# Expert attention of a four-stage model on one core: norm spread over three engines, lead-in and tail reordered

## What is computed

```python
ss = sigmoid(x @ Ws).reshape(b, t, H, E); sd = sigmoid(x @ Wd).reshape(b, t, H, E)
ms, md = topk_mask(ss, 3), topk_mask(sd, 3)
q = einsum('bthed,bthe->bhtd', q5, sd * md)       # q5, k5, v5: x @ Wq, x @ Wkv
k = einsum('bthed,bthe->bhtd', k5, ss * ms)
v = einsum('bthed,bthe->bhtd', v5, ss * ms)
out = softmax(q * DH ** -0.5 @ k.T) @ v
o5 = einsum('bthd,dm->bthm', out, Wo).reshape(b, t, H, E, DIM)
y = einsum('bthem,bthe->btm', o5, md)
x = layernorm(x + y)                              # (x - mean) / sqrt(var + 1e-5)
```

## Time and profile before

| | us |
|---|---|
| median of 3 runs | 2145.1 |
| the profiled execution | 2147.77 |
| its span, first to last instruction | 2145.9 |
| lead-in of the expert attention (end of the block before to the first exponential, L669) | 279.5 to 362.4 |
| its 32 periods | 362.4 to 1368.0 |
| its tail (to the flag) | 1368.0 to 1423.2 |

### The profile page before, as it was taken

One profiled execution on the slowest core, in us unless ns is written; L12 is line 12 of the kernel. 1 busy time (PEld: TensorE's weight loads), 2 busy tenths in 40 slices (PEclk: granted clock), 3 DMA queues, 4 the chain that ended last, 5 costly groups with the idle time before them and its releaser, 6 DMA issues. The chain is left out here.

```text
span 2145.9 us, 25496 instructions
## 1 busy us (share of the span) xinstructions
PE 1807.0 (84%) x8678; PEld 817.6 (38%) x8678; DVE 1255.9 (59%) x2012; ACT 1245.2 (58%) x2372; POOL 892.6 (42%) x446
## 2 busy tenths in 40 slices
PE   5667718999999989999899999546999999999386
PEld 2323315544555444554445453112233332333143
DVE  5898949797667877688777566222213313120277
ACT  0000012676776666776666767604999999999232
POOL 3333311687876777767777678700000000000000
PEclk9988759999999999999999999756999999999688
DMA  1000010000000000000000000013220302200001
GB/s 37 10 10 0 0 32 10 19 19 10 19 19 19 10 19 10 19 19 10 19 10 19 19 10 1 0 31 118 70 75 34 111 28 79 79 20 21 21 30 39
DMA packets 28345, 60.50 MB, mean 28 GB/s; under 512 B 4210, under 2 KB 14900, under 8 KB 28212
## 3 DMA queue, kind: packets, MB, share of 16 engines
q1 hardware_dynamic: 28212, 58.81, 8.4%
HBM read 37.83 MB, written 18.87 MB: 26 GB/s over the span
## 5 line engine op out<-in xcount | busy, mean ns | idle before, releaser
L549 POOL TENSOR_TENSOR b_psum<-b_psum,b_probs 128x1024 f32<-128x1024 f32 x192 | 460.3, 2397 | 195.9 <-ACT b_probs L669 189.6
L1784 ACT ACTIVATE c_probs<-banks 128x1024 f32<-128x1024 f32 x512 | 484.3, 1040 | 72.0 <-PE banks L1836 49.1
L1022 DVE TENSOR_TENSOR b_gated<-banks,b_g 128x480 f32<-128x480 f32 x512 | 313.3, 655 | 222.3 <-PE banks L764 217.4
L669 ACT ACTIVATE b_probs<-banks 128x1024 f32<-128x1024 f32 x256 | 254.1, 1018 | 243.5 <-PE banks L797 242.5
L764 PE MATMUL banks<-b_w,b_xh 128*128 128x480 f32 x1024 | 350.1, 397 | 32.8 <-DVE b_xl L967 17.0
L797 PE MATMUL banks<-b_qq,b_kk 64*128 64x512 f32 x1024 | 266.6, 628 | 34.6 <-DVE b_gated L1022 28.3
L1030 DVE TENSOR_REDUCE b_tok<-b_gated 128x192 f32<-128x960 f32 x256 | 281.4, 1138 | 0.5
L1851 PE MATMUL banks<-c_probs,c_vg 128*32 128x512 f32 x2048 | 277.4, 614 | 5.1 <-DVE c_acc L1946 3.3
L646 ACT ACTIVATE b_share<-b_o,b_picked 128x64 f32<-128x64 f32 x1120 | 278.3, 337 | 4.2 <-DVE b_o L1055 4.0
L829 PE MATMUL banks<-b_probs,b_tok 128*64 128x512 f32 x1024 | 255.9, 622 | 0.9 <-ACT b_probs L669 0.9
L764 PEld LDWEIGHTS banks<-b_w,b_xh 128*128 128x128 f32 x1024 | 193.8, 189 | 112.8 <-issue 57.0
(11 more groups left out here) (195 smaller groups left out, 1877.9 us busy)
## 6 DMA issues: line engine op xcount, KB each, us to landing
b_raw_w<-in_L_ffn_W SPq DMA_DIRECT2D x32, 480.0 KB, 3.2
c_heads<-c_split SPq DMA_DIRECT2D x24, 512.0 KB
c_keys<-c_heads SPq DMA_DIRECT2D x16, 512.0 KB, 3.7
c_queries<-c_heads SPq DMA_DIRECT2D x16, 512.0 KB, 4.7
c_heads<-c_split SPq DMA_DIRECT2D x8, 384.0 KB
a_xs<-in_L_attn_x SPq DMA_DIRECT2D x4, 512.0 KB, 3.8
d_xs<-r SPq DMA_DIRECT2D x4, 512.0 KB, 2.9
out<-d_yo SPq DMA_DIRECT2D x4, 512.0 KB, 3.2
```

The costliest lines, as they stand in the source:

```text
L549: nc.gpsimd.tensor_tensor(psum[:, par, :], prev, probs[:, i % 4, :], ALU.add).then_inc(psum_rdy, 1)
L669: nc.scalar.activation(probs[:, i % 4, :], score_b[i % 2], ACT.Exp).then_inc(exp_rdy, 1)
L1022: nc.vector.tensor_tensor(shape(gated[:, t % 2, j, :]), shape(proj_b[u % WAYS][:, 0:HALF_W]), g.unsqueeze(2).broadcast_to([P, 3, HD2, E]), ...
L1784: nc.scalar.activation(probs[:, step % 2, c, :, :], unit_b[u % NU], ACT.Exp, scale=float(HD) ** -0.5).then_inc(exp_rdy, 1)
```

## The change

- **Norm of batches 0 to 2**: VectorE does the statistics, the variance plus eps and the first guess (`moment_parts`, in h = 4 and 5). GpSimd does the Newton steps and a shift -mean * rs, 14 dependent steps on [128 x 8] (`inverse_roots`, in h = 6 after i = 3). ScalarE scales: eight activations out = Identity(rs * y + shift) (`finish_norm`, in h = 7 at p = 1).
- **Lead-in**: Wo is loaded behind the raw weights of heads 0 and 1, under a semaphore of its own. TensorE waits for nothing before it turns x, for Ws and Wd before the gates, and for the memsets before the keys. ScalarE copies the turned x, takes the gates' exponentials and splits x ahead of the casts of the weights; VectorE does its split ahead of the gates.
- **Tail**: the shares of head 31 are 40 `scalar_tensor_tensor` on VectorE, straight into z, each half released by itself. The ten steps go to ten different banks and to separate copies in the memory of probs and psum. The count of safe reciprocals comes ahead of the norm. The last norm stays wholly on VectorE.
- Five more semaphores for each of the two calls of `switch_attention`.

```diff
@@ -423,6 +423,7 @@
...
+        shift = sb("shift", [P, NT])
...
@@ -442,9 +443,11 @@
...
+        moments, newton, normed, z_last = map(sem, ("moments", "newton", "normed", "z_last"))
...
+        last_b = [ps[:, 2 + k, :] for k in range(6)] + [ps[:, k, :] for k in range(4)]
...
@@ -505,17 +516,18 @@
...
-                for e in range(E):
-                    at = DH * (e % 2)
-                    sp.dma_start(wo[at:at + DH, e // 2, :], I["L0_ffn_Wo"][:, e * D:(e + 1) * D]).then_inc(w_in, 16)
...
-                for n in range(3):
+                for n in range(2):
...
+                for e in range(E):
+                    at = DH * (e % 2)
+                    sp.dma_start(wo[at:at + DH, e // 2, :], I["L0_ffn_Wo"][:, e * D:(e + 1) * D]).then_inc(wo_in, 16)
+                weights(2, 2)
@@ -562,6 +574,8 @@
...
+                        if i == 3 and norm_last and h == 6:
+                            inverse_roots(b - 1)
@@ -569,12 +583,24 @@
...
+                def inverse_roots(b):
+                    pool.wait_ge(moments, MOMENT_STEPS * (b + 1))
+                    st = Steps(pool, newton, NEWTON_STEPS * b)
+                    var, half_step = tmp[:, 0, :], tmp[:, 1, :]
+                    for _ in range(3):
+                        st.link(nc.gpsimd.tensor_tensor(half_step, rs[:, :], rs[:, :], ALU.mult))
+                        st.link(nc.gpsimd.tensor_tensor(half_step, half_step, var, ALU.mult))
+                        st.link(nc.gpsimd.tensor_scalar(half_step, half_step, -0.5, 1.5, ALU.mult, ALU.add))
+                        st.link(nc.gpsimd.tensor_tensor(rs[:, :], half_step, rs[:, :], ALU.mult))
+                    st.link(nc.gpsimd.tensor_tensor(shift[:, :], mv[:, :, 0], rs[:, :], ALU.mult))
+                    st.done(nc.gpsimd.tensor_scalar(shift[:, :], shift[:, :], -1.0, None, ALU.mult))
+                    assert st.n == NEWTON_STEPS, st.n
...
-                for half in range(2):
-                    add_share(half, B * NH - 1, B - 1, NH - 1)
...
@@ -649,6 +675,12 @@
...
+                def finish_norm(b):
+                    act.wait_ge(newton, NEWTON_STEPS * (b + 1))
+                    for t in range(NT):
+                        nc.scalar.activation(out[:, b * NT + t, :], y[:, t, :], ACT.Identity, bias=shift[:, t:t + 1], scale=rs[:, t:t + 1]).then_inc(normed, 1)
@@ -695,17 +727,20 @@
...
+                        if p == 1 and h == 7 and norm_last:
+                            finish_norm(b - 1)
...
+                for r in range(2):
+                    turned_x(0, r)
+                for r in range(2):
+                    gate_exps(0, r)
+                split_x(0)
...
-                for work in (turned_x, gate_exps):
-                    for r in range(2):
-                        work(0, r)
-                split_x(0)
@@ -713,10 +748,13 @@
...
-                for t in range(0, NT, 2):
-                    gated_share(last_n, B - 1, NH - 1, (t, t + 1))
-                for k in range(OUT_STEPS):
-                    copy_out(B - 1, k)
+                for k in range(6):
+                    act.wait_ge(zT_ps, ZT0 + OUT_STEPS * (B - 1) + k + 1)
+                    n_rows = min(P, ED - k % 3 * P)
+                    nc.scalar.copy(last_z(k // 3)[0:n_rows, k % 3, :], last_b[k][0:n_rows, :]).then_inc(zT_sb, 1)
+                for half in range(2):
+                    act.wait_ge(zT_ps, ZT0 + OUT_STEPS * (B - 1) + 7 + half)
+                    nc.scalar.copy(last_y(half), last_b[6 + half]).then_inc(zT_sb, 1)
@@ -732,6 +770,7 @@
...
+                        pe.wait_ge(w_in, 16 * 2)
...
@@ -927,14 +967,13 @@
...
-                pe.wait_ge(w_in, 16 * (2 + E))
-                pe.wait_ge(clear, 2)
...
+                pe.wait_ge(clear, 2)
@@ -946,12 +985,31 @@
...
-                for k in range(OUT_STEPS):
-                    out_left(B - 1, k)
-                    project_out_step(B - 1, k)
-                out_left(B - 1, OUT_STEPS)
+                pe.wait_ge(mult, MULT0 + U * B * NH)
+                pe.wait_ge(exp_rdy, EXP0 + NT * B * NH)
+                pe.wait_ge(wo_in, 16 * E)
+                for k in range(6):
+                    half, c = k // 3, k % 3
+                    n_rows = min(P, ED - c * P)
+                    if c == 0:
+                        pe.wait_ge(z_last, ED // DH * 4 * (half + 1))
+                    for j in range(4):
+                        flat = z[:, (B - 1) % 2, 4 * half + j, :, :].rearrange("p e d -> p (e d)")
+                        last = nc.tensor.transpose(last_b[k][0:n_rows, j * P:(j + 1) * P], flat[:, c * P:c * P + n_rows], ident[:, :])
+                    last.then_inc(zT_ps, 1)
+                for half in range(2):
+                    pe.wait_ge(zT_sb, Z_COPIES * (B - 1) + 3 * half + 3)
+                    for c in range(3):
+                        n_rows = min(P, ED - c * P)
+                        last = nc.tensor.matmul(last_b[6 + half], wo[0:n_rows, c, :], last_z(half)[0:n_rows, c, :], start=(c == 0), stop=(c == 2))
+                    last.then_inc(zT_ps, 1)
+                for half in range(2):
+                    pe.wait_ge(zT_sb, Z_COPIES * (B - 1) + 7 + half)
+                    for j in range(4):
+                        last = nc.tensor.transpose(last_b[8 + half][:, j * P:(j + 1) * P], last_y(half)[:, j * P:(j + 1) * P], ident[:, :])
+                    last.then_inc(zT_ps, 1)
...
-                    turn_counts(nc, pe, judged, good, ident, turn_b[0:1, 0:P])
+                    turn_counts(nc, pe, judged, good, ident, last_b[2][0:1, 0:P])
...
@@ -1055,12 +1112,49 @@
...
-                def norm_parts(b):
+                def moment_parts(b):
...
-                    st = Steps(dve, norm_steps, ONE + NORM_STEPS * b)
-                    yield from layer_norm_parts(nc, st, y, out[:, bass.ds(b * NT, NT), :], stats, mv, rs, tmp)
-                    st.settle_apart()
-                    assert st.n == NORM_STEPS
+                    if b:
+                        dve.wait_ge(newton, NEWTON_STEPS * b)
+                        dve.wait_ge(normed, NT * b)
+                    st = Steps(dve, moments, MOMENT_STEPS * b)
+                    for half in range(2):
+                        for t in range(4 * half, 4 * half + 4):
+                            st.done(nc.vector.bn_stats(stats[:, t, :], y[:, t, :]))
+                        yield
+                    st.settle()
+                    for t in range(NT):
+                        st.done(nc.vector.bn_aggr(mv[:, t, :], stats[:, t, :]))
+                    yield
+                    st.settle()
+                    st.link(nc.vector.tensor_scalar(tmp[:, 0, :], mv[:, :, 1], LN_EPS, None, ALU.add))
+                    st.done(nc.vector.tensor_scalar(rs[:, :].bitcast(I32), tmp[:, 0, :].bitcast(I32), -0.5, float(0x5F3759DF), ALU.mult, ALU.add))
+                    assert st.n == MOMENT_STEPS, st.n
+                    yield
+                def last_shares(n):
+                    for half in range(2):
+                        dve.wait_ge(z_rdy[half], Z0 + n)
+                    dve.wait_ge(o_rdy, O0 + n + 1)
+                    b, h = n // NH, n % NH
+                    for t in range(NT):
+                        for e in range(E):
+                            nc.vector.scalar_tensor_tensor(z[:, b % 2, t, e, :], o[:, t, :], picked[:, b % 2, t, h * E + e:h * E + e + 1], z[:, b % 2, t, e, :], ALU.mult, ALU.add).then_inc(z_last, 1)
+                def last_norm(b):
+                    dve.wait_ge(normed, NT * b)
+                    dve.wait_ge(newton, NEWTON_STEPS * b)
+                    for half in range(2):
+                        dve.wait_ge(zT_ps, ZT0 + OUT_STEPS * b + 9 + half)
+                        some = slice(4 * half, 4 * half + 4)
+                        nc.vector.tensor_tensor(y[:, some, :], last_b[8 + half].rearrange("p (t c) -> p t c", t=4), x[:, b * NT + 4 * half:b * NT + 4 * half + 4, :], ALU.add).then_inc(y_rdy, 1)
+                    dve.wait_ge(y_rdy, 2 * b + 2)
+                    st = Steps(dve, norm_steps)
+                    layer_norm(nc, st, y, out[:, b * NT:(b + 1) * NT, :], stats, mv, rs, tmp)
+                    st.settle()
@@ -1074,7 +1168,7 @@
...
-                        waiting["norm"] = norm_parts(b - 1)
+                        waiting["norm"] = moment_parts(b - 1)
@@ -1099,21 +1193,18 @@
...
-                        if norm_last and h >= 4 and p % 2:
-                            next(waiting["norm"], None)
+                        if norm_last and h in (4, 5) and p % 2:
+                            next(waiting["norm"])
...
-                    if norm_last and h == NH - 1:
-                        for _ in waiting["norm"]:
-                            pass
...
+                split_x(0)
...
-                split_x(0)
@@ -1123,13 +1214,12 @@
...
-                for half in range(2):
-                    add_residual(B - 1, half)
-                for _ in norm_parts(B - 1):
-                    pass
```

(6 more changed lines are left out.)

14 lines of the change are left out of this document (9 added, 5 removed).

## The result

The changed kernel takes 2090.5 us in the median of four runs (2083.62 to 2095.73), against 2144.8 for the kernel before (four runs, 2138.58 to 2145.93): the ratio is 0.9746, 95% interval 0.9726 to 0.9767. That is 54.3 us less, where 48.5 were forecast, and 6.1 us under the forecast time of 2096.6. The profiled execution is the fastest of the four: 2083.62, span 2081.8, mean granted clock 0.942 (before: 2147.77, 2145.9 and 0.923).

The account below looks back on a forecast made before the run. No engine saturated throughout; TensorE bounds undisturbed heads, GpSimd the last ones. Lead-in 13.5, steady heads 20.9 and tail 14.1 sum to 48.5 us: 2147.8 to 2099.3 profiled, median 2096.6, range 2082 to 2115.

Parts of the forecast that it names:

- Cause of the long heads: Heads h = 6, 7, batches 1 and 2: GpSimd stretches VectorE's small norm steps, TensorE waits; moving them gains 23.9 us.
- GpSimd's steps: Norm in h = 6: 14 dependent steps on GpSimd at 0.36 us each, together N = 5 us (3.5 to 7).
- N - 3.5: Batches 1 and 2: TensorE's wait for the low weights (L538) queued behind GpSimd's steps, 1.5 us each, 3.0 in all.
- rival (e): GpSimd's norm steps are cheap, 3.5 us together: 4.5 us more gained, 2092 us; chance 12%.
- Rival (a): VectorE holds up GpSimd's small norm steps as GpSimd does VectorE's; at 2 us a step 2165.6 us, slower; chance 3%.
- Lead-in: Block start to first gating: no wait for Wo, reordered work, one collision of 2.1 us; gain 13.5 us (11 to 15.7).
- Last batch: Last heads: GpSimd is the bound, so its norm steps delay the last share of head 30 by 3.5 us (1.5 to 6).
- Tail: After the last shares: VectorE shares, separate banks, clock rising between two projections, earlier count; gain 14.1 us, semaphore clears charged 0.7.
- Rival (c): The clock stays at 1.2 GHz in the tail: 4.6 us less gained, 2101 us; chance 16%.
- (b): GpSimd's norm steps are merely dear, 0.55 us each, and ScalarE's eight activations outlast their cover: 2107 us; chance 17%.
- (d): Loads or both L538 hold the gates in the lead-in: up to 4 us less gained, 2100.5 us; chance 12%.
- (f): Idle time in h = 6 and 7 returns as another wait and the tail gains nothing: within 0.2%; chance 2%.

Follow-up runs that it names:

- `after_again`: The changed kernel, unchanged, timed again beside the kernel before on one chip: 2087.7 us, ratio 0.972.
- `last_roots_again`: Second run of the changed kernel with the 14 steps of batch 2's norm moved from GpSimd to VectorE in the last batch: 2081.4 us, ratio 0.9707.

## Why the prediction came out right, step by step

**Cause of the long heads: right.** With the small steps gone h = 6 and 7 fell to 29.4, and with GpSimd's sums cut short they fell there while VectorE kept all its work. 24.0 us came back in these four heads, the whole of the forecast's 23.9. L75 or L76 is still held in h = 5 (2.3 us in batches 1 and 2) and costs nothing there, as I had put it.

**GpSimd's steps: mis-sized, by 1.1 us.** N was put at 5 us and is 3.9, since a step costs 0.28 and not 0.36: the gap, 0.08, was lost in the difference of two large numbers (0.13), and the length is 0.20. That my lower end for the length, 0.19, lies so near it is luck: the copy's 238 ns less 56 columns at 2.02 ns is 0.125, not 0.19. The wait forecast as N - 3.5 came as 0.23 at N = 3.9, where that is 0.4, and as 6.87 at N = 10.7, where it is 7.2. With so small a wait nothing is left of the 3.0 us that were charged for batches 1 and 2. In this term rival (e), cheap steps, was nearer than the forecast.

**Rival (a) fell, but the argument against it was too broad.** GpSimd's steps run beside L1079 and L1087 of VectorE or beside nothing, and keep to 0.19 to 0.24. I had argued that GpSimd's sums keep to 2.35 to 2.46 whatever VectorE does; over all of them, that is not so (2.34 to 2.75, last section). None of the steps met a VectorE operation of the kind that holds GpSimd. Nor did a first call cost anything: the first `tensor_scalar` on GpSimd takes 0.20. The Trainium skill ("GPSIMD Engine Reference", Instruction dispatch) gives about 6 us for the first call of a freshly loaded routine; this trace doesn't show it here.

**ScalarE: hidden, as forecast, though over its bound.** The eight activations take 3.2 us against 2.0 to 2.9 (the 0.36 of the upper end came from no row; they take 0.40 each), and ScalarE's busy time in h = 7 goes from 21.3 to 24.3 us; the head stays at 29.4. On VectorE the same work cost 3.8 a head.

**Lead-in: right in its steps, 1.3 short in its sum.** First gating 28.7 us after the block's start, as forecast; one collision of 2.0 us, as forecast (L1043 takes 6.83 for eight, 4.81 in the kernel before, where nothing is beside it). The gain at this point is 13.2. But 12.25 is what arrives at the first exponential: between gating and exponential the kernel after takes 41.9 us, the one before 40.9. The clock is the likely cause. In this trace it is at 0.5 once more for 3.4 us, from 342.9, with TensorE busy throughout, shortly before the first exponential at 349.55. Of the nine traces with the new lead-in the five that have this dip reach the first exponential after 70.5 to 70.7 us, the four without it (`after_again` among them) after 69.0 to 69.2, which would be a gain of 13.6 to 13.8.

**Last batch: near in number, half right in its reason.** The delay, forecast as 3.5, is 2.9 in this trace (55.03 less 52.13) and 2.3 in the second (54.42). The steps do hold back GpSimd's last sum of head 30, from 22.7 to 25.95 us after that head's start, and through TensorE's row sums the work behind it. But GpSimd is not the engine that comes last in the trace I read: it idles 0.9 us for ScalarE's exponential before its last sum in the kernel before, and 0.7 in the kernel after. ScalarE's chain is about as long.

**Tail: mis-sized by 4.** The gain from GpSimd's last share of head 30 to the end was put at 14.1 net of the 3.5; it is 21.0 less 2.9, 18.1. Three pieces make up the 4.0. From the last share to the statistics I had 21.3 us (1379.6 to 1400.9) and it is 19.1: 2.2, and that is the clock. I let it rise between the two projections, 5.78 and then 2.9; it rose before both, and the twelve matmuls took 6.29, 2.4 less. The 40 shares were right (7.93 against 8.1), the transposes ended 0.7 earlier, the two rounds took 0.9 longer. The delay was 0.6 shorter. And from the statistics to the next block 2.3 us came back where I had 1.2, since the ten more semaphore clears, charged with 0.7, show in no run: from the flag to the next block it is 12.9 us before and 12.3 after. Rival (c), no rise, is refuted for this tail; with one bank both projections did run at 0.50.

**The other rivals.** (b) fell with N = 3.9 and h = 7 at 29.4, (d) with the first gating at 28.7, (f) with the four heads at 29.4 and the tail's gain.

**Sum.** 12.25 + 24.0 + 18.1 is 54.4, and h = 4, whose length varies from execution to execution (31.71, 34.11 and 35.09 in one trace of the kernel after, 34.74, 35.09 and 34.12 in the other), adds 0.4 in these two traces: 54.8. The three terms were 13.5, 20.9 and 14.1: one too large by 1.3, two too small by 3.1 and 4.0. So the mechanisms held, and the sum was 6 us too cautious, mostly by the wait charged to the steps and by the clock in the tail.

## What to carry to other kernels

Price a small VectorE instruction with its inputs in the memory that GpSimd uses by what GpSimd does beside it, not by its size; either give it to an engine that isn't held, or place one such instruction in each slack slot and never several ahead of work that TensorE waits for. A long pause of TensorE can cost more than its length, since the clock follows (6.87 us cost 8.7 here, while 0.23 cost nothing). Chained steps through one bank ran the tail's projections at half clock here, and steps from separate banks ran them at full clock.

## What the runs showed of the hardware that I had not expected

**Some operations of VectorE and GpSimd hold each other, whichever starts first.** In the timeline of `last_roots_again` above the eight-column steps of VectorE take 0.17 or 2.3 us in turn: each held one ends with one of GpSimd's sums (1293.95 and 12.33 for five, so 2.47 each: 1296.42, 1298.88 and so on). GpSimd waits too. All instructions of line L561 in the kernel after, columns as in rows 3, then a timeline with the longest of them (the second of the pair) and VectorE's operation beside it:

```profile
L561 POOL TENSOR_TENSOR b_psum<-b_psum,b_probs x192: 2337/2384/2750, 355.4 to 1333.7; 128x1024 f32<-128x1024 f32 x192
```

```profile
696.05 5.28 POOL L561 TENSOR_TENSOR b_psum<-b_psum,b_probs 128x1024 f32<-128x1024 f32 x2 [0.84 <-ACT b_probs L701]
...
696.43 2.70 DVE L1043 TENSOR_TENSOR b_beats<-b_gate 128x512 bf16<-128x512 f32 x1
```

L1043 starts 0.38 us into GpSimd's first sum, is held to its end, and finishes at 699.13, which holds the second sum: the pair takes 5.28 in place of 4.90. Seven of the eight sums above 2.6 us begin while an L1043 is under way, the eighth during a `tensor_scalar` of 640 columns (L1032). Reciprocals (L1036, 1094 to 1155 ns over all 16), reductions (L1087, 1100 to 1164 over 256) and operations that read a bank (L1079, 635 to 662 in 511 of 512, 895 in one) keep their length. The Trainium skill ("SBUF — State Buffer", SBUF: two separate sides) has this as a lock on a pair of ports that the two engines share, taken for a whole instruction by GpSimd or by a VectorE operation with two inputs in that memory or in a two-port mode; the traces agree on which operations are held and until when.

**Steps of eight columns on GpSimd are cheap**: 0.28 us each with the gap, against 0.20 on a VectorE that is left alone (L79 to L81 in the tail) and 1.9 to 2.8 on one that is held (L79 to L81 in the kernel before).
